# A four-block network on one core: the GELUs of both token halves between one pair of activation-table loads

## The reference, cut to what matters

```python
h = modulate(layernorm(x))
q, k, v = split(h @ Wqkv + b)              # layer 1, 2: q and k are also rotated (cos, sin)
attn = softmax(q @ k.T * scale)            # 16 heads, 512 x 512 each
x = x + gate1 * (attn @ v @ Wo + bo)
h = modulate(layernorm(x))
x = x + gate2 * (gelu(h @ W1 + b1) @ W2 + b2)
```

## Time and profile before

| what | value |
|---|---|
| median of 3 runs | 419.15 us |
| lowest, highest | 415.48, 419.73 us |
| the profiled execution's own time | 417.63 us |
| its span in the trace | 415.7 us |
| EXP tiles on ACT, first start to last end | about 35.4 to 375.6 us |
| busy share of the span PE, DVE, ACT, POOL | 93%, 79%, 78%, 45% |
| ACT_TABLE_LOAD, all lines | 27 |

### The profile page before, as it was taken

The page is one execution under the profiler, slowest core; times in us unless marked ns, Lnnn a source line. Parts: engine busy times, 40 slices in busy tenths (PEclk is TensorE's granted clock), DMA queues, the critical chain, the costliest instruction groups (busy, mean ns, idle before and its releaser), DMA issues. The chain is left out here.

```text
span 415.7 us, 10244 instructions
## 1 busy us (share of the span) xinstructions
PE 388.4 (93%) x3666; PEld 205.8 (49%) x3670; DVE 329.4 (79%) x768; ACT 323.8 (78%) x634; POOL 187.5 (45%) x290
## 2 busy tenths in 40 slices
PE   8699899999999999999999998999999999998996
PEld 3444343455544544554545544545555444435874
DVE  6497999989886499898899874899898889935343
ACT  5207786799898968887989887769797999895664
POOL 4539999525745155453162354171451320004564
PEclk9759999999999999999999998999999999999999
DMA  7700237210005000013000023000050000000001
GB/s 254 184 15 14 78 113 203 72 32 2 2 2 149 7 6 2 2 53 103 3 6 2 2 56 98 6 2 2 2 135 20 3 2 16 2 0 3 2 0 39
DMA packets 17186, 17.63 MB, mean 42 GB/s; under 512 B 2460, under 2 KB 15454, under 8 KB 17120
## 3 DMA queue, kind: packets, MB, share of 16 engines
q1 hardware_dynamic: 15840, 16.19, 13.8%
q10 hardware_dynamic: 1296, 0.79, 0.8%
HBM read 6.62 MB, written 0.52 MB: 17 GB/s over the span
## 5 line engine op out<-in xcount | busy, mean ns | idle before, releaser
L1397 DVE TENSOR_REDUCE mx<-max_ps 128x1 f32<-128x512 f32 x384 | 241.9, 682 | 30.3 <-PE max_ps L908 29.2
L1223 ACT ACTIVATE probs<-exp_ps 128x512 f32<-128x512 f32 x384 | 202.6, 605 | 29.4 <-PE exp_ps L917 28.3
L908 PE MATMUL max_ps<-k_stack,q_stack 64*128 64x512 bf16 x384 | 113.5, 390 | 6.9 <-DMA k_stack<-parts 3.5
L1098 PE MATMUL pv_ps<-probs,v_ones 128*32 128x256 f32 x1536 | 103.0, 385 | 4.5 <-ACT probs L1223 3.8
L917 PE MATMUL exp_ps<-q_stack,k_stack 64*128 64x256 bf16 x768 | 101.3, 271 | 0.6 <-ACT probs L1223 0.5
L1417 POOL TENSOR_SCALAR var_eps<-mv 128x2 f32<-128x2 f32 (+2 forms) x33 | 6.5, 198 | 131.1 <-DVE mv L1257 130.0
L1098 PEld LDWEIGHTS pv_ps<-probs,v_ones 128*32 128x32 f32 x1536 | 41.1, 109 | 42.7 <-ACT probs L1223 17.2
L908 PEld LDWEIGHTS max_ps<-k_stack,q_stack 64*128 64x128 bf16 x384 | 29.4, 93 | 61.9 <-DVE mx L1397 36.2
L917 PEld LDWEIGHTS exp_ps<-q_stack,k_stack 64*128 64x128 bf16 x768 | 43.3, 94 | 29.4 <-ACT probs L1223 11.5
L1235 ACT ACTIVATE mrows<-exp_ps 8x256 bf16<-8x256 bf16 x48 | 17.5, 365 | 17.5 <-PE exp_ps L1083 17.1
L1030 PE MATMUL exp_ps<-hT,w 128*128 128x256 f32 x96 | 29.3, 425 | 0.8 <-ACT hT L1157 0.8
(11 more groups left out here) (128 smaller groups left out, 485.1 us busy)
## 6 DMA issues: line engine op xcount, KB each, us to landing
k_stack<-parts SPq DMA_DIRECT2D x36, 128.0 KB, 2.5
q_stack<-parts SPq DMA_DIRECT2D x30, 128.0 KB
w<-in_w_dram SPq DMA_DIRECT2D x4, 448.0 KB, 3.3
w<-in_w_dram SPq DMA_DIRECT2D x4, 256.0 KB, 2.9
w<-in_ada_dram SPq DMA_DIRECT2D x1, 896.0 KB, 5.2
w<-in_rows_dram SPq DMA_DIRECT2D x1, 832.0 KB, 7.4
q_stack<-mrows SPq DMA_DIRECT2D x48, 4.0 KB
x<-in_x_dram SPq DMA_DIRECT2D x2, 256.0 KB, 3.5
```

Of the source, the lines that this page charges most:

```text
L908: return pe.matmul(max_bank(n), half(q_stack, b, pair, j)[:, t * P:(t + 1) * P], half(k_stack, b, pair, j), start=True, stop=True)
L1098: mm = pe.matmul(pv_ps[32 * j:32 * j + 32, cols_of(g // 2)], v_ones[:, b, kt, 4 * g + j, :], probs[:, (4 * i + j) % RING_P, cols_of(of_two ...
L1223: act.activation(probs[:, tile % RING_P, :], exp_bank(e), ACT.Exp, scale=SCORE_SCALE[hc // 2 // NB]).then_inc(exp_read, 1)
L1397: dve.tensor_reduce(mx[:, G % 2, t, 2 * (pair % 2) + j:2 * (pair % 2) + j + 1], max_bank(n), AX_X, ALU.max, negate=True).then_inc(max_read, 1)
```

## The change

In jobs 2 to 5 the GELUs of both halves share one window: half 0's first `W1` is not placed before both halves' inputs (`TR`) are, half 1's first `W1` not before half 0's last, and the window stays open from half 0's first to half 1's last. `SIN` goes behind half 1's. Jobs 6 and 7 keep a window for each half. Three numbers of the scheduler change as well: the due time of batch 1's first norm, POOL's lead time, and the slack of `ROWS`.

```diff
-SECOND_BATCH = 5.0
+SECOND_BATCH = 9.0
...
-AHEAD = {"DVE": 1.15, "ACT": 0.1, "POOL": 1.65, "SP": 0.95}
-SLACK = {"ROWS": -0.8, "DENSE": -0.3, "PV": 0.85, "ANG": 0.1, "EXP": 0.1, "MAX": 0.8, "NEAR": 0.15, "BESIDE": 0.5, "ALONE": 0.25, "CHANGE": 0.2, "LAST": 0.4}
+AHEAD = {"DVE": 1.15, "ACT": 0.1, "POOL": 1.45, "SP": 0.95}
+SLACK = {"ROWS": -1.0, "DENSE": -0.3, "PV": 0.85, "ANG": 0.1, "EXP": 0.1, "MAX": 0.8, "NEAR": 0.15, "BESIDE": 0.5, "ALONE": 0.25, "CHANGE": 0.2, "LAST": 0.4}
...
-        if (k, w) == (NB, "W1") and h == 0:
+        if (k, w) == (NB, "W1") and h == 1:
             names.append("SIN")
...
-            if window[0] not in (None, (name, k, h)):
+            if window[0] not in (None, (name, k)):
                 return None
-            return need({"W1": ("TR", k, h, 0), "W1S": ("MK", k, h, 0), "W1F": ("TR", k, h, 2)}[name],
-                        *([("RED", 3, WHOLE, 0)] if (k, h) == (NB, 0) else [("SIN", 0, WHOLE, 0)]))
+            both = pieces_of(k) if k < CHAINS else (h,)
+            if h == 1 and k < CHAINS and c == 0 and ("W1", k, 0, CHUNKS[name] - 1) not in at:
+                return None
+            return need(*[{"W1": ("TR", k, hh, 0), "W1S": ("MK", k, hh, 0), "W1F": ("TR", k, hh, 2)}[name] for hh in both],
+                        *([("RED", 3, WHOLE, 0)] if k == NB else [("SIN", 0, WHOLE, 0)]))
...
-                window[0] = (name, k, h) if c < CHUNKS[name] - 1 else None
-                if (k, h) == (NB, 0) and name == "W1":
-                    window[0] = (name, k, h)
+                window[0] = (name, k) if c < CHUNKS[name] - 1 or k < CHAINS and h == 0 else None
+                if k == NB:
+                    window[0] = (name, k)
```

## The result

| what | before | changed |
|---|---|---|
| median, lowest to highest of 20 runs each | 417.25 us, 415.48 to 420.04 | 421.06 us, 419.31 to 422.45 |
| ratio changed to before | | 1.0077, 95% interval 1.006 to 1.0095 |
| profiled execution, span | 417.63, 415.7 us | 419.72, 417.8 us |
| end of the last EXP tile in the trace | 375.6 us | 377.7 us |

The changed kernel is slower, by 0.77%: real, but under the 1% that the prediction counts as change.

A forecast was written before the change was run, and what follows sets the result against it. No engine alone was taken as the bound, but PE, DVE and ACT waiting in a ring. Terms -5.1 + 3.7 + 1.6 + 0.8 = +1.0 us on 419.15 gave 420.2 us, range 413 to 428.

The forecast's parts named there:

- no measurable change: The forecast case: what ACT gives up is mostly waited away again; 420.2 us, own range 416 to 424, chance 0.44.
- the ring: In the stretch of the exponentials, 35.4 to 375.6 us, PE, DVE and ACT wait for each other; none is full.
- Table loads: ACT, jobs 2 to 5: eight loads of 1.283 us go, 10.3 us, of which half counts: -5.1 us.
- By the chain's half: Three of job 6's six loads lie on the chain of waits, so half of ACT's saved load time counts: -5.1 us.
- One block of K and Q work: Jobs 2 and 4: half 0's MLP waits for half 1's input, POOL's last split comes later: +3.7 us.
- I take the middle: Later copies of jobs 2 and 4: between 0, all in the room, and 7.5 us, none in it: +3.7 us.
- Gaps lose their filling: GELUs in DVE's gaps before half-chains 4 and 8 move among dense MAX tiles: +1.6 us, bounds 0 to 3.1.
- Start and clock: Eight WARM matmuls go; PE's clock may rise late, stretching 30 to 34 us: +0.8 us, bounds 0 and +4.
- SLACK and AHEAD: A few places in the order shift by one or two tiles, 0.5 to 1.6 us each way; taken as 0.
- POOL's: Rival: POOL's block in jobs 2 and 4 delays the next attention; 424.0 to 428.3, say 426 us, chance 0.28.
- ACT nearer the bound: Rival: half the loads count and the room takes the later copies; 414.0 us, 408.9 with all loads, chance 0.20.
- the clock did fall low at the start: Rival: PE's clock stays low at the start, +4 in place of +0.8: 423.4 us, chance 0.08.

The follow-up runs named there:

- loads_out: Kernel before, order untouched, sixteen GELUs of jobs 2 to 5 replaced by the identity so that eight table loads go: 417.67 us, ratio 1.001.
- loads_back: Changed kernel, its order kept, exponential's table brought in behind half 0's fourth GELU of jobs 2 to 5, eight loads back: 423.63 us, ratio 1.0144.
- E7.24: Not a run and without a measured time: a place in the order, EXP tile 24 of half-chain 7.
- The old start: Changed kernel, with the order of before, including WARM, up to the first EXP tile of half-chain 2: 421.25 us, ratio 1.0076 to the kernel before.
- after_to_e9: Changed kernel's order up to the first EXP tile of half-chain 9, then what is left in the order of before: 422.60 us, ratio 1.0118.

## Why the prediction was right or wrong

The time, 420.2 us, lies 0.9 us from the 421.06 measured, and "no measurable change" was the case that came. That it is so near is luck: the base was 1.9 us too high (419.15 for 417.25) and the change 2.8 us too small (+1.0 us forecast, +3.8 measured between the medians; by the ratio 0.77%, 3.2 us). And within the change, terms of both signs cancelled that were too large. What was right is the ring: time taken from ACT is waited away again. By its terms:

- **Table loads, -5.1 us: mis-sized, should have been near 0.** The failing step is "By the chain's half". The chain's three windows were job 6's, none of the eight windows that the change touches. With the order held fixed, taking the eight loads out gave a ratio of 1.001 (loads_out), and put into the merged order they cost 2.6 of 11.1 us by the medians, 1.7 by the traces (loads_back). "If it is under 336 us, the loads were on the path" was the right test: 342.3. The argument for the forecast, that what ACT gives up is mostly waited away again, is what ACT's waits show (28.3 to 34.2 us in loads_out).
- **One block of K and Q work, +3.7 us: the delay came, its price did not.** The last split ended 6.9 us later after the window's begin than before, within the 4.8 to 8.0 of the step; 30 us was forecast, 32.1 it was. The step that failed is "I take the middle" between room and no room. First MAX tile of half-chain 8 0.4 us earlier, of half-chain 4 1.3 later: about 0. The test named for it (gap equal or shorter if the room takes it) came out that way, 4.68 for 5.19. But the row read for the size of the room, 260.46 less 256.2, holds W1 products at the lower clock, 1.5 us longer than at the higher. And the new place of the MAX tile, E7.24, is seven EXP tiles behind the copies, not eight.
- **Gaps lose their filling, +1.6 us: about 0.** From the end of half-chain 4 to that of 8, with two merged windows on the way, the changed kernel gains 1.3 us. The loads, POOL and the filling all lie there, so the trace gives only their sum: forecast at +0.2 for the four jobs, measured -0.5 at the end of half-chain 8, of which up to 1.5 us is the low clock of before at 255 us. What I missed is that a merged window has a wait of 1.7 to 2.0 us inside it.
- **Start and clock, +0.8 us: about 0 in the profiled execution, and the test did not see what happened.** "The rise owed most to the gates' products" is true of the rise, which came without `WARM` and no later (0.68 over 29 to 30 us, 0.52 before). The test "PEclk at 1.00 by 30 to 31 us" came out right (1.00), and yet the start was not: the clock fell back to 0.50 from 33 to 40 us, a case that the prediction does not have. Half-chain 0 ends 0.2 us later and half-chain 1 0.9 us earlier all the same. The old start brought nothing back (1.0076 beside 1.0077), but it did not raise the mean clock either; where the low clock lasted from 15 to 42 us it cost 2.5 us (after_to_e9).
- **SLACK and AHEAD, "I take 0": the step that failed by most.** Half of the change is these three numbers. Alone they cost 1.95%; without them the merged windows cost 2.6%; and the order that they and the windows give behind half-chain 9 costs 0.6% when it is put behind the order of before, 1.7 us of it at one place (PV 93 ahead of EXP tile 24). "0.5 to 1.6 us each way" is the size of one such place; how many there are was not counted, and in these three orders they did not average out.

The Trainium skill's figure, 2.66 us a switch (page "ScalarE: Activation LUTs", section "What ACT_TABLE_LOAD costs"), would have made, as an estimate, -10.6 us. The loads here are 1283 ns with 0.01 to 0.02 us around them in the changed kernel too (283.59 + 1.28, next exponential at 284.88), so the measurement decides against the drain; and taking eight switches away gave no gain at all, 1.001 (0.9983 to 1.0037).

The rivals: POOL's had the sign right and the mechanism not (the later copies were not paid); ACT nearer the bound fell with loads_out; the clock did fall low at the start, at a cost of about 0 in the one execution that the trace shows.

**Open.** The profiled executions differ by 2.1 us and the medians by 3.8. The 1.7 us between go with the clock: the trace of the changed kernel is of one of its faster executions, at 0.975, and 12 of the 20 are at 0.972 or less, 1.6 us longer in the mean. Where in those the clock is low no trace shows. That PV 93's place costs 1.7 us is read from traces, with and without it, and not tried by moving it alone. The 0.9 us that arise besides between the ends of half-chain 8 and of tile 23 of half-chain 11 are not explained.

## What to carry to other kernels

Where three engines wait for each other in a ring, do not count time taken from one that has waits on either side as won until a run with the order held fixed shows it; the share of a chain counts only for the very instructions that lie on it. An edit to a list scheduler is two edits, the work that it removes and the order that comes out, and here the second was the larger (up to 2.6%): splice the old and the new order at a few places to see where the time arises. Merging two windows saves the length of one only if all that the second reads is ready in time; here other work of PE stood between. A test that delays one engine delays all that stands behind it there: read in the trace which of them was waited for before crediting the one it was meant for. And compare two traces with their granted clocks beside them.

## What the runs showed of the hardware that I had not expected

- TensorE's granted clock fell back after it had risen. In the changed kernel it was 0.88 over 30 to 34 us, then 0.50 over 34 to 38 with PE shown busy 4.00 of 4.00 us. Such stretches at 1.2 GHz stand in the middle of most of the traces, in the kernel before at 255.2 to 258.7 us, behind 252 to 255 with PE busy 1.97 of 3.00 us. There eight matmuls took 3.47 us that took 1.99 at 2.4 GHz.
- A table load stands against its neighbours without a gap (0.01 to 0.02 us), and PE and DVE went on through it: during the load from 276.67 to 277.95 PE began four W1 matmuls (277.14) and DVE a MAX tile (277.24), and taking eight away left their busy time as it was (325.0 and 326.0, 287.0 and 288.0 us).
